# GpSimd's pacing waits begin with the second group and ask for work of the step under way

## What is computed

```
h = relu(layernorm(x));  hW = h @ W.T
e = leaky_relu(a_src[src] + a_dst[dst])            # 8 heads
alpha = exp(e - segment_max(e, dst)) / segment_sum
x = x + segment_sum(alpha * hW[src], dst) + bias   # layer 0

h = relu(layernorm(x));  q, k, v = h @ Wq, h @ Wk, h @ Wv (+ biases)
score = (q[dst] . k[src]) / 4 + edge_attr @ We + be
alpha = softmax over the edges of one dst
x = x + layernorm(segment_sum(alpha * v[src], dst) @ Wo + bo + h) * gamma + beta
```

## Time and profile before

| | us |
|---|---|
| runs of the kernel before | 1632.68, 1634.03, 1643.87 (median 1634.03) |
| the profiled execution, its own time | 1644.29 |
| its span in the trace | 1642.3 |
| busy: TensorE (PE) | 1022.8 (62%) |
| busy: VectorE (DVE) | 927.7 (56%) |
| busy: GpSimd (POOL) | 900.2 (55%) |
| busy: ScalarE (ACT) | 640.9 (39%) |

### The profile page before, as it was taken

How to read it: one execution, slowest core, us unless ns; L and a number is a source line. 1 busy time by engine, 2 the same in 40 slices (tenths; PEclk the granted TensorE clock), 3 DMA queues, 4 the chain that set the end, 5 groups by cost and what they waited for, 6 DMA issues and landing times. The chain is left out here.

```text
span 1642.3 us, 21266 instructions
## 1 busy us (share of the span) xinstructions
PE 1022.8 (62%) x4985; PEld 859.9 (52%) x4985; DVE 927.7 (56%) x3002; ACT 640.9 (39%) x1699; POOL 900.2 (55%) x926
## 2 busy tenths in 40 slices
PE   5237666676676666767451766756676675766675
PEld 4126555454464554655341655646565575655564
DVE  6136555565565655556810656565656656556567
ACT  5233442433434334341350543434344443443414
POOL 5735565666666666662056356565566666666500
PEclk9555555555555555555675767687776767776765
DMA  6212221222222222122243122222222222223201
GB/s 135 73 38 51 51 58 48 59 58 50 61 55 51 58 50 56 44 47 70 58 120 88 39 78 85 83 77 81 78 86 82 85 82 82 84 82 86 77 1 40
DMA packets 56923, 110.35 MB, mean 67 GB/s; under 512 B 17421, under 2 KB 31393, under 8 KB 56677
## 3 DMA queue, kind: packets, MB, share of 16 engines
q0 software_dynamic: 36288, 91.12, 21.0%
q1 hardware_dynamic: 19203, 17.39, 3.8%
q10 hardware_dynamic: 1313, 0.50, 0.1%
HBM read 100.60 MB, written 8.81 MB: 67 GB/s over the span
## 5 line engine op out<-in xcount | busy, mean ns | idle before, releaser
L504 POOL DMA_INDIRECT G<-table,idx_all x880 | 873.8, 993 | 578.8 <-issue 240.5
L832 PE MATMUL bank<-PV,S 128*125 128x144 f32 x1760 | 488.4, 428 | 84.2 <-DVE acc L1409 41.9
L1409 DVE TENSOR_TENSOR acc<-acc,bank 125x144 f32 x880 | 260.5, 296 | 371.2 <-PE bank L832 224.9
L832 PEld LDWEIGHTS bank<-PV,S 128*125 128x125 f32 x1760 | 384.0, 289 | 111.2 <-issue 67.2
L608 ACT ACTIVATE S<-iota_n,lid 128x125 f32<-128x125 f32 x880 | 275.7, 386 | 0.7 <-issue 0.7
L817 PE MATMUL bank<-qe,ST 125*128 x880 | 151.4, 335 | 117.9 <-DVE prod L1209 104.8
L817 PEld LDWEIGHTS bank<-qe,ST 125*128 125x128 f32 x880 | 142.3, 247 | 126.6 <-issue 126.4
L618 ACT ACTIVATE ST<-bank 125x512 f32<-125x512 f32 x110 | 65.1, 597 | 275.3 <-PE bank L804 141.2
L1387 DVE TENSOR_TENSOR PV<-G,PV 128x512 f32<-128x512 f32 x220 | 151.0, 687 | 21.7 <-issue 19.1
L612 ACT ACTIVATE S<-S,ones 128x500 f32<-128x500 f32 x220 | 156.6, 712 | 11.2 <-ACT S L608 4.1
L1199 DVE TENSOR_SCALAR ST<-bank,vcol 125x512 bf16<-125x512 f32 x110 | 81.6, 742 | 106.1 <-remote 90.0
(11 more groups left out here) (219 smaller groups left out, 1126.8 us busy)
## 6 DMA issues: line engine op xcount, KB each, us to landing
G<-table,idx_all POOLq DMA_INDIRECT x880
prod<-in_edge_attr_dram SPq DMA_DIRECT2D x26, 224.0 KB
table<-G SPq DMA_DIRECT2D x12, 224.0 KB
bias_rows<-qe SPq DMA_DIRECT2D x1, 1664.0 KB
table<-h0b SPq DMA_DIRECT2D x8, 178.5 KB
out_dram<-G SPq DMA_DIRECT2D x8, 168.0 KB
prod<-in_edge_attr_dram SPq DMA_DIRECT2D x26, 30.0 KB
xs<-in_x_dram SPq DMA_DIRECT2D x1, 504.0 KB
```

Of the source, the lines that this page charges most:

```text
L504: pool.indirect_dma_start(G[:, u, v, 0:w], None, table, bass.IndirectOffsetOnAxis(ap=idx_all[:, g * GV + v:g * GV + v + 1], axis=0)).then_ ...
L832: pe.matmul(ms[p % 2][0:BN, k * 256:k * 256 + H * SLOT], S[:, ur, 2 * p + k, :], PV[:, 2 * p + k, :, :].rearrange("p h k -> p (h k)"), sta ...
L1409: ve.tensor_tensor(a, a, o, ALU.add).then_inc(s.sem["acc_added"], 1)
```

## The change

`pace` changes in four ways. It acts from the first group on: in group 0 visit 12 waits for `t_done` 4, in both layers. Groups 1 and 2 get the waits of the later ones, without those on `mm_done`. In layer 0 visit 8 asks for `hop1` where it asked for `scoreT`, and visit 12 for `hop2` where it asked for `hop1`, all of step g. In layer 1 visits 4, 8 and 12 asked for signals of step g-1, and ask for those of step g: `hop1` and the second transposes, `hop2` and the third transposes, the second expansion. The waits on `mm_done` stay. Apart from this, `bias_parts` moves from step 29 to step 27 of layer 0.

```diff
--- before.py
+++ after.py
@@ -462,33 +462,44 @@
             def pace(n, g, v):
 
                 s, r, q = L[n], g - UNROLL, g - 1
-                if r < 0 or v % 4:
+                if v % 4:
+                    return
+                if g == 0:
+                    if v == 12:
+                        wait(pool, s["t_done"], 4)
                     return
                 if n == 0:
                     if v == 0:
                         wait(pool, s["expanded"], 4 * q + 2)
-                        wait(pool, s["mm_done"], GV * r + 9)
+                        if r >= 0:
+                            wait(pool, s["mm_done"], GV * r + 9)
                     if v == 4:
                         wait(pool, s["expanded"], 4 * q + 4)
-                        wait(pool, s["mm_done"], GV * r + 14)
+                        if r >= 0:
+                            wait(pool, s["mm_done"], GV * r + 14)
                     if v == 8:
-                        wait(pool, s["scoreT"], g)
-                        wait(pool, s["mm_done"], GV * r + 16)
+                        wait(pool, s["hop1"], g)
+                        if r >= 0:
+                            wait(pool, s["mm_done"], GV * r + 16)
                     if v == 12:
-                        wait(pool, s["hop1"], g)
-                        wait(pool, s["mm_done"], GV * r + 20)
+                        wait(pool, s["hop2"], g)
+                        if r >= 0:
+                            wait(pool, s["mm_done"], GV * r + 20)
                 else:
                     if v == 4:
-                        wait(pool, s["hop1"], q)
-                        wait(pool, s["mm_done"], GV * r + 4)
+                        wait(pool, s["hop1"], g)
+                        wait(pool, s["t_done"], 4 * g + 2)
+                        if r >= 0:
+                            wait(pool, s["mm_done"], GV * r + 4)
                     if v == 8:
-                        wait(pool, s["hop2"], q)
-                        wait(pool, s["t_done"], 4 * q + 3)
-                        wait(pool, s["mm_done"], GV * r + 8)
+                        wait(pool, s["hop2"], g)
+                        wait(pool, s["t_done"], 4 * g + 3)
+                        if r >= 0:
+                            wait(pool, s["mm_done"], GV * r + 8)
                     if v == 12:
-                        wait(pool, s["expanded"], 4 * q + 3)
-                        wait(pool, s["t_done"], 4 * q + 4)
-                        wait(pool, s["mm_done"], GV * r + 12)
+                        wait(pool, s["expanded"], 4 * g + 2)
+                        if r >= 0:
+                            wait(pool, s["mm_done"], GV * r + 12)
 
             def gathers(n, table, w):
                 s = L[n]
@@ -1409,7 +1420,7 @@
                         ve.tensor_tensor(a, a, o, ALU.add).then_inc(s.sem["acc_added"], 1)
 
 
-                    if n == 0 and g == GROUPS + 1:
+                    if n == 0 and g == GROUPS - 1:
                         bias_parts()
                     node_rows(0)
                     load_offsets(0)
```

## The result

The changed kernel is slower: 1798.84 us (median of four, 1784.89 to 1815.97) against 1636.97, a ratio of 1.0969 with the 95% interval 1.0881 to 1.1057. The slowest of the four was in a slower state of the chip and is left out of the ratio. The forecast was 1735, 6% slower.

The account below looks back on a forecast made before the run. Waits bound the kernel: long uninterrupted gather runs withhold other engines' signals. Terms -18 + 10 - 22 + 130 + 0 = +100 on the profiled 1644.3 gave 1744, on the median's scale 1735 us; range 1595 to 1860.

Parts of the forecast that it names:

- What bounds the kernel: Whole kernel: waits, not engine throughput or clock, set the step; 19.0 us is free, the rest is the runs' price.
- stops: Spells in long gather runs when other engines' signals reach nobody, from 7.3 to 10 us in until about 3 us after the last start.
- Layer 0's start: Layer 0's first steps: first score transpose at 70 instead of 101.37, steps 1 and 2 longer by 13; net -18 us.
- Layer 1's start: Layer 1's first steps: first score transpose at 870, 38 us sooner, steps 1 and 2 longer by 12 and 4; net -22.
- Layer 0's steady steps: Layer 0's 24 later steps: runs stay twelve and four gathers, +0.4 us a step, +10 in all.
- D: Rival for layer 0's steady steps: `hop2` splits runs into eight and eight, -80 instead of +10, 1645 us; chance 0.14.
- B: Rival: both layers fall into runs of sixteen gathers, 1852 us; chance 0.13.
- Layer 1's steady steps: Layer 1's 24 later steps: one run of sixteen gathers, a step of 31.0 us, +130 in all, from +77 to +182.
- The data chain: Layer 1's steady steps: the last quarter's gather lands late, so the next score transpose isn't before +25.7 us of the step.
- bias_parts: Its move from step 29 to 27 of layer 0: covered by stops or only moved, 0 us, from -3 to +3.
- Rival C: Both layers: stops don't grow with a run's length, layer 1's step is bound by data alone, 1591 us; chance 0.20.
- test for contention at a shared interface: VectorE's two-input addition takes 0.30 us with or without gathers under way, so no contention between GpSimd and VectorE shows.

Follow-up runs that it names:

- pause8_b: Kernel before, with GpSimd clearing an unused tile twice ahead of every eighth of layer 1's first 48 gathers; 1628.30 us, 0.9881 of the kernel before.
- v0_gate_b: Changed kernel plus a wait in layer 1 from group 3: visit 0 asks for its own step's score transpose; 1686.08 us, 1.0235 of the kernel before.
- l1_v4_prev: Changed kernel, but layer 1's visit 4 asks for the previous step's hop 1 and no transposes; 1849.16 us, 1.1234 of the kernel before.
- l0_only: Kernel before, with the changed waits of layer 0 only, for groups 3 and later; 1682.31 us, 1.0228 of the kernel before.
- l1_only: Kernel before, with the changed waits of layer 1 only, for groups 3 and later; without stops 1464.13 us, 1.1053 of the kernel before.

## Why the prediction was right

**What bounds the kernel: right, on chips with stops.** Breaking the runs without changing any dependence speeds the kernel up (pause8_b). A wait that lets the run of sixteen end 4.6 us sooner in the step makes the changed kernel faster (v0_gate_b), and an eased one that lets it end later makes it slower (l1_v4_prev). Longer runs go with longer steps inside one execution (l0_only), which by itself shows no cause. Four things in my reading were wrong. Signals don't reach "nobody" in a run: some come through late (1203.51 above). Layer 0 had three steps of eight and eight, of 22.7, 26.3 and 22.1 us, and not one. Layer 1's steps were not always eight and eight, but in 21 of 24. And I took the stops for a property of every execution, and on the other chips they are absent. There my reading of the kernel before would have been wrong: in layer 1 its steps are bound by GpSimd's 20 us, and 19.0 is no free step.

**Layer 0's start**, -18: measured -18.6. **Layer 1's start**, -22: measured -23.8. The first transposes came at 61.8 (taken 70) and 31 us after the first gather (taken 35), and the two steps behind them cost more than I took (57 us for layer 0's pair instead of 49). The errors cancel, so that both sums fit this well is luck.

**Layer 0's steady steps**, +10: measured +13.0 in that profile and up to +30 in others. That 13 is so near 10 is in part luck too. I had the old breaks at visits 12 and 0 stay; they went, and the new ones are at visit 8 and at 4 or 0 or nowhere. Twelve and four came in 14 of 24 steps, D's eight and eight in 6 and B's sixteen in 3, though D's way there, a break by `hop2` at visit 12, didn't. The price that I gave the run of sixteen, a step of 30.8, was 28.6 in the mean.

**Layer 1's steady steps**, +130, from +77 to +182: measured +172. The mechanism was right in its parts, one run of sixteen from +6.8 (+6.7) to +25.6 (+26.3). The mis-sized term is what follows the run. I let signals come back 2.7 us after the last start and the next transpose 0.5 us after that; it was 3.4 and 2.8, because a sum, a product, a sum and the addition of scores all wait in VectorE's queue behind the held addition. 26.3 + 3.4 + 2.8 = 32.5. Where in the run the stop begins, on which I spent two bounds (7.3 and 10 us), hardly counts; its end does. The upper end of 33.2 was a good bound, and I weighed it down with a factor from steps of another shape. These 42 us are most of the 64 by which 1735 was too low. Most of the rest is scatter: the changed kernel's profiled execution took 14 us less than its median, that of before 7 more.

**The data chain**, "not before +25.7": right, and l1_only shows it bare, at +26.2. In the changed kernel with stops it is hidden behind them. The part of the change that makes data late is thus a loss of its own: with stops 7.2 us a step by the run's end, without them 5.7 by the data. The rule to issue a DMA early, which the Trainium skill states ("DMA: Bandwidth & Descriptors", Rules for kernel authors) and which I left out of the sum, agrees with l1_only.

**bias_parts**, 0: the stretch that holds it took 84.7 us instead of 86.4, and in three other profiles with the stops and the move 85.3 to 85.7, in three without the move 84.6 to 86.0. Nothing can be told, as forecast.

**Rival C** (runs cost nothing, 1591, faster) is refuted with stops. Without them its premise is true, and yet the change is slower there too, since the step of before is then 20.5 and not 25.6: C took the steady price of late data from a step that the stops had already lengthened. Its point of decision, a step of layer 1 under 27 us, was met without stops, with the opposite sign of the result. The prediction's test for contention at a shared interface took the wrong instruction. VectorE's addition has one of its two inputs in PSUM (`bank`), and its mean of 296 ns before and after says little. The weighing L1398 has both in SBUF, and beside it the gather is the longer one: 1.65 us instead of 0.95 (1194.22 and 1194.37 above), while the weighing takes its usual 0.67 to 0.69. Chips without stops show this too (1.65 us at 1004.06 in l1_only), and 0.7 us on GpSimd don't make a wait of 8 to 13 us on the other engines.

## What to carry to other kernels

If one engine issues gathers back to back, look in the timeline at what the others do in the run's second half and in the 3 us behind it. Idle time ended by "remote", often on several engines together, is the run's price where there are stops, and there an earlier end of the run, or a break in it, can be worth more than earlier data. A pacing wait can be paid twice, by the data that come late behind it and by everything that queues up behind it in one run; count both from the next signal that the step needs. Look at the runs' shapes in the timeline before a change in them is called the cause: v0_gate_b had the time that I expected for runs of twelve, with runs of sixteen. And measure on more than one chip, and at more than one time, before a bound is called a property of the hardware.

## What the runs showed of the hardware

- Two kinds of chips: one and the same kernel took 1320 to 1327 us on two chips and 1628 to 1652 on three others. All idle time that "remote" ended behind 37 us is on the latter. What makes the kinds, and whether they are of the chip or of the moment, is open.
- With stops, most of the long waits in runs of sixteen began 9 to 18 us into the run and ended 3 to 4 us after its last start, often on two engines at once. A rest of 3.95 us in which GpSimd clears a tile twice lets signals pass; the transfers end in it too. Whether 2.2 us do wasn't measured with stops. The path by which a run of gathers holds signals between other engines wasn't found.
- Without stops 48 gathers in a row held nobody, and from the start of a quarter's last gather (visit 15, at 1014.76 in l1_only) to the product that waits for it at 1017.46 it was 2.7 us.
- A gather beside a VectorE instruction with both inputs in SBUF took 1.65 us of GpSimd's time instead of 0.95 (1194.22 in the changed kernel).
